# Mamba recurrence of a four-layer network: chunks of 64 tokens, two side by side on the partitions, in place of chunks of 128

## What is computed

```python
dt = softplus(dt + dt_bias)
a  = exp(dt * -exp(A_log))                      # one decay per token and head
db = dt[..., None, None] * x[..., None] * Bh[:, :, :, None, :]
states = associative_scan(a2*s1 + s2, (a, db))  # along the tokens
y = einsum('blhps,blhs->blhp', states, Ch) + D_param * x
y = y * silu(z); y = group-normed over 256 features; out = y @ W_out + b_out
```

## Time and profile before

| | |
|---|---|
| median of 3 runs | 2790.08 us (2783.35 to 2790.38) |
| the profiled execution: own time, span | 2787.64 us, 2785.9 us |
| PE busy | 2633.5 us (95% of the span), 13426 matmul records |
| DVE (VectorE) busy | 1671.9 us (60%) |
| ACT (ScalarE), POOL (GpSimd) busy | 1069.7 us (38%), 944.4 us (34%) |
| mean granted TensorE clock | 0.973 of full speed |

### The profile page before, as it was taken

The page is one execution under the profiler, slowest core; times in us unless marked ns, Lnnn a source line. Parts: engine busy times, 40 slices in busy tenths (PEclk is TensorE's granted clock), DMA queues, the critical chain, the costliest instruction groups (busy, mean ns, idle before and its releaser), DMA issues.

```text
span 2785.9 us, 35158 instructions
## 1 busy us (share of the span) xinstructions
PE 2633.5 (95%) x13426; PEld 1670.9 (60%) x13426; DVE 1671.9 (60%) x3408; ACT 1069.7 (38%) x1954; POOL 944.4 (34%) x921
## 2 busy tenths in 40 slices
PE   7988988999999999999999998889999999979996
PEld 4445544664656556566566565646666666756896
DVE  6676672227575664755763324678888988844323
ACT  2534552114444443544444112433444444332221
POOL 3221210003232231322321003426767767754222
PEclk8999999999999999999999999979999999989998
DMA  6222211017000000000000200000000000035123
GB/s 189 62 61 64 60 46 61 0 46 105 1 1 1 1 1 1 1 1 1 0 16 1 105 0 31 1 16 12 16 16 12 16 13 16 13 125 191 58 73 135
DMA packets 57112, 109.11 MB, mean 39 GB/s; under 512 B 13792, under 2 KB 32480, under 8 KB 55792
## 3 DMA queue, kind: packets, MB, share of 16 engines
q1 hardware_dynamic: 53152, 96.47, 12.4%
q0 software_dynamic: 3792, 10.39, 1.0%
HBM read 71.16 MB, written 27.08 MB: 35 GB/s over the span
## 4 chain that ended last, share of the span: by engine, by line
PE 87%; DVE 7%; ACT 2%; issue 1%; DMA 1%; POOL 1%; SPq 1%; POOLq 0%; DVEq 0%; ACTq 0%
PE ps L1256 9%; PE ps L1238 8%; PE ps L1771 5%; PE ps L1247 5%; PE ps L1228 5%; PE ps L1812 4%; PE ps L378 4%; PE ps L1265 4%; PE ps L360 4%; PE ps L365 4%; PE ps L1874 4%; PE ps L2889 3%; PE ps L2913 3%; PE ps L697 2%; PE ps L721 2%; PE ps L1840 2%
## 5 line engine op out<-in xcount | busy, mean ns | idle before, releaser
L1256 PE MATMUL ps<-back 128*128 128x512 f32 x576 | 292.0, 596 | 0.3 <-ACT back L1299 0.3
L1299 ACT ACTIVATE back<-ps 128x512 f32<-128x512 f32 x288 | 170.1, 597 | 266.2 <-PE ps L1247 264.5
L1294 ACT ACTIVATE back<-ps,front 128x128 f32<-128x128 f32 (+7 forms) x256 | 189.1, 739 | 71.7 <-DVE front L1345 70.0
L1388 POOL TENSOR_TENSOR back<-back 128x512 f32<-128x512 f32 x72 | 91.4, 1270 | 362.0 <-DVE back L1333 361.9
L1247 PEld LDWEIGHTS ps<-front,back 128*128 128x128 f32 x1152 | 140.8, 141 | 118.4 <-issue 95.0
L1398 POOL TENSOR_SCALAR back<-back,front 128x128 f32<-128x128 f32 (+5 forms) x192 | 142.5, 746 | 191.3 <-DVE front L1364 188.5
L809 ACT ACTIVATE back<-ps 128x1024 f32<-128x1024 f32 (+1 forms) x192 | 150.8, 811 | 128.2 <-PE ps L721 127.7
L1345 DVE TENSOR_REDUCE front<-ps 128x1 f32<-128x128 f32 (+7 forms) x256 | 194.0, 758 | 8.8
L1974 DVE TENSOR_TENSOR_SCAN back<-ps,back 128x512 f32<-128x512 f32 x128 | 155.9, 1218 | 50.4 <-PE ps L1784 50.1
L1338 DVE TENSOR_TENSOR ps<-ps,front 128x128 f32<-128x128 f32 x256 | 76.1, 297 | 165.8 <-PE ps L1238 165.8
L1247 PE MATMUL ps<-front,back 128*128 128x128 f32 x1152 | 170.5, 273 | 3.4 <-DVE back L1370 3.4
(11 more groups left out here) (319 smaller groups left out, 5694.1 us busy)
## 6 DMA issues: line engine op xcount, KB each, us to landing
whole<-l_w SPq DMA_DIRECT2D x32, 512.0 KB, 5.2
front<-back SPq DMA_DIRECT2D x128, 64.0 KB, 2.0
rounded<-qh SPq DMA_DIRECT2D x28, 256.0 KB
rounded<-kh SPq DMA_DIRECT2D x56, 128.0 KB
front<-xg SPq DMA_DIRECT2D x47, 129.0 KB
xg<-front SPq DMA_DIRECT2D x2, 3008.0 KB, 35.8
front<-l_win SPq DMA_DIRECT2D x1, 4640.0 KB, 17.7
front<-l_wgu SPq DMA_DIRECT2D x2, 2048.0 KB, 13.5
```

What stands on the lines that cost most here:

```text
L1256: e.matmul(PS[:, 7, :], self.V[:, j, G % 4 * 128:G % 4 * 128 + 128], self.turned(("turn", n, j)), start=(j == 0), stop=(j == qt)).then_inc ...
L1294: e.activation(self.P[n % 2][:, h, :nk], s[:, :nk], ACT.Exp, bias=st[:, 0, h:h + 1], scale=1.0, accum_out=st[:, 1, h:h + 1]).then_inc(A.se ...
L1299: e.activation(self.turned(step), self.bank(step), ACT.Copy).then_inc(A.sem, 1)
```

## The change

The chunks get 64 tokens. Two chunks of 64 (s = 0, 1) that were one chunk of 128 lie on partitions 0 to 63 and 64 to 127 of LT, XD, Bd and CB, so each table of decays is 64 x 64 and LT, CB and the scan's width are halved. There are 8 states per n instead of 4, kept in 8 buffers.

- scan: two steps per n instead of four, each two matmuls of 256 columns (one per head) into one bank and one scan of 128 x 512. New weights `selA` pick a chunk's half for each half of the partitions; GpSimd builds them together with `selP` (for cp), 768 columns per two n instead of 128, at an earlier place.
- cb: 8 matmuls with 64 columns of weights and 64 moving instead of 4 of 128 x 128. The copy and the products with LT have half the width.
- st: 8 chunks, weights 64 x 32, in two steps: s = 0 at place 0.05, s = 1 at 0.2, with a gate and an out step between them. h waits for the second.
- within: two steps of 16 matmuls (weights 64 x 64, 64 columns moving), at 0.25 and 0.35, with xd, cb and a gate step between them.
- across: 8 chunks of 64 columns. h: 8 instructions instead of 4, the same size each.
- cp: two matmuls of 256 columns instead of one of 512.
- `MambaSteps`: eight copies of 32 x 256 and sixteen scans of 64 x 64. The identity is built with one instruction instead of four.

```diff
         "pe": {"raw": (-2.5, -2),
-             "scan": (-1.1, -1, -0.8, -0.6), "st": (0.05,), "within": (0.25,), "across": (0.6,),
+             "scan": (-1.1, -0.8), "st": (0.05, 0.2), "within": (0.25, 0.35), "across": (0.6,),
...
         "dve":
-             "scan": (-1, -0.8, -0.65, -0.5), "h": (0.2, 0.3, 0.3, 0.5),
+             "scan": (-1, -0.65), "h": (0.2, 0.2, 0.3, 0.3, 0.3, 0.3, 0.5, 0.5),
...
             elif kind == "scan":
-                e.matmul(p, m.pair[:, hh:hh + 1].broadcast_to([128, 128]), m.R[:, tok], start=True,
-                         stop=True).then_inc(P.sem, 1)
+                for j in range(2):
+                    t = e.matmul(p[:, 256 * j:256 * j + 256], m.selA[g % 2][:, 2 * step[2] + j, :], m.Ra[:, cols],
+                                 start=True, stop=True)
...
             elif kind == "cb":
-                    t = e.matmul(p[:, i * 128:i * 128 + 128], m.BC[q, g // 4, o], m.BC[q, 2 + g // 4, o], start=True,
+                    for s in range(2):
+                        t = e.matmul(p[64 * s:64 * s + 64, i * 64:i * 64 + 64], m.BC[q, g // 4, o],
+                                     m.BC[q, 2 + g // 4, o], start=True, stop=True)
...
             elif kind == "st":
+                q = slice(64 * s, 64 * s + 64)
                     for h in range(4):
-                        t = e.matmul(S[32 * h:32 * h + 32, i, :], m.Bd[:, i, h, :],
+                        t = e.matmul(S[32 * h:32 * h + 32, 2 * i + s, :], m.Bd[q, i, h, :],
...
             elif kind == "within":
                     for h in range(4):
+                        s = h // 2 if step[2] == 0 else 1 - h // 2
+                        q = slice(64 * s, 64 * s + 64)
-                        t = e.matmul(net.PS[r, self.Y[h // 2], v], m.XD[:, c, h * 64:h * 64 + 64], m.LT[:, h, c, :],
+                        t = e.matmul(net.PS[r, self.Y[h // 2], v], m.XD[q, c, h * 64:h * 64 + 64],
+                                     m.LT[q, c4, h, i, :], ...)
...
             elif kind == "across":
-                for i in range(4):
+                for i in range(8):
...
             elif kind == "h":
-                w.wait_ge(self.products, self.pn["st", n])
+                w.wait_ge(self.products, self.pn["st", n, 1])
```

More of the change, by code:

```diff
@@ L1439, in __init__ @@
         self.Crep = sb(WA0 + 15936, 1024)
-        self.sel = [net.sbr(R0 + 128 * i, 128) for i in range(2)]
-        self.ident4 = sb(EX0, 512)
+        self.ident8 = sb(EX0, 512)
         self.dt = sb(EX0 + 512, 16, 32)
@@ L1496, in __init__ @@
         self.wide = net.sb(WA0 + 13376 + 512 * 5, 512)
-        self.rows = net.sb(WA0 + 16448, 2048)
+        self.rows = net.sb(WA0 + 16448, 1024)
     def pe_begin(self, e, w):
@@ L1630 @@
     AT = {
-        "pe": {"raw": (-2.5, -2), "scan": (-1.1, -1, -0.8, -0.6), "xd": (-0.75, -0.6), "cp": (-0.2,),
-             "cb": (-0.74,), "st": (0.05,), "within": (0.25,), "across": (0.6,), "gate": (0.15, 0.3), "var": (1.45,),
+        "pe": {"raw": (-2.5, -2), "scan": (-1.1, -0.8), "xd": (-0.75, -0.6), "cp": (-0.2,),
+             "cb": (-0.74,), "st": (0.05, 0.2), "within": (0.25, 0.35), "across": (0.6,), "gate": (0.15, 0.3), "var": (1.45,),
              "out": (1.85, 2.2)},
@@ L1781, in pe @@
             elif kind == "scan":
-                hh = 4 * g + step[2]
                 p = self.take(w, step, self.B)
-                e.matmul(p, m.pair[:, hh:hh + 1].broadcast_to([128, 128]), m.R[:, tok], start=True,
-                         stop=True).then_inc(P.sem, 1)
+                w.wait_ge(self.pooled, self.gn["sel", n // 2 * 2])
+                for j in range(2):
+                    t = e.matmul(p[:, 256 * j:256 * j + 256], m.selA[g % 2][:, 2 * step[2] + j, :], m.Ra[:, cols],
+                                 start=True, stop=True)
+                t.then_inc(P.sem, 1)
             elif kind == "xd":
@@ L1795, in pe @@
                 p = self.take(w, step, self.B)
-                w.wait_ge(self.pooled, self.gn["sel", n // 2 * 2])
-                e.matmul(p, m.sel[g % 2], m.R[:, tok], start=True, stop=True).then_inc(P.sem, 1)
+                for s in range(2):
+                    t = e.matmul(p.rearrange("p (i s t) -> p s i t", i=4, s=2)[:, s], m.selP[g % 2][:, s, :],
+                                 m.Rp[:, cols], start=True, stop=True)
+                t.then_inc(P.sem, 1)
             elif kind == "cb":
@@ L1831, in pe @@
                 w.wait_ge(self.results, self.dn["xd", n, 1])
+                if step[2]:
+                    w.wait_ge(P, self.pn["within", n, 0])
                 if n > 0:
@@ L1972, in dve @@
                 if n > 1:
-                    w.wait_ge(self.products, self.pn["within", n - 2])
-                e.tensor_tensor_scan(m.LT[:, h, four, :].rearrange("p a b -> p (a b)"), self.bank(step, self.B),
-                                     m.ident4, 0.0, ALU.mult, ALU.add).then_inc(D.sem, 1)
+                    w.wait_ge(self.products, self.pn["within", n - 2, 1])
+                e.tensor_tensor_scan(m.LT[:, c4, 2 * h:2 * h + 2].rearrange("p h a b -> p (h a b)"), self.bank(step, self.B),
+                                     m.ident8, 0.0, ALU.mult, ALU.add).then_inc(D.sem, 1)
             elif kind == "xd":
@@ L1989, in dve @@
                     w.wait_ge(self.products, self.pn["across", n - 2])
-                    for i in range(4):
+                    for i in range(8):
                         if not self.last_chunk(n - 2, i):
                             w.wait_ge(D, self.dn["h", n - 2, i])
-                e.tensor_copy(m.ach[:, four], p[:, 127:512:128])
+                e.tensor_copy(m.ach[:, 8 * c4:8 * c4 + 8], p[:, 63:512:64])
                 w.wait_ge(self.crep[c4], 64 * (n // 2 + 1))
@@ L1996, in dve @@
             elif kind == "bd":
-                for h in range(4):
+                for h in range(2):
                     w.wait_ge(D, self.dn["scan", n, h])
@@ L2012, in dve @@
                 st = self.state(n, i)
-                w.wait_ge(self.products, self.pn["st", n])
-                if st > 3:
-                    w.wait_ge(self.products, self.pn["across", self.reader(st - 4)])
-                new, old = m.H[st % 4], m.H[(st - 1) % 4]
+                w.wait_ge(self.products, self.pn["st", n, 1])
+                if st > 7:
+                    w.wait_ge(self.products, self.pn["across", self.reader(st - 8)])
+                new, old = m.H[st % 8], m.H[(st - 1) % 8]
                 if c4 + i == 0:
@@ L2068, in pool @@
                     w.wait_ge(self.products, self.pn["cp", n - 3])
-                e.tensor_copy(m.sel[g % 2].rearrange("p (a b) -> p a b", a=4),
-                              m.pair[:, 32 + 4 * g:36 + 4 * g].unsqueeze(2).broadcast_to(
-                                  [128, 4, 32])).then_inc(G.sem, 1)
+                both = m.pair.rearrange("p (s h) -> p s h", s=2)[:, :, 4 * g:4 * g + 4]
+                e.tensor_copy(m.selA[g % 2].rearrange("p h (s t) -> p h s t", s=2),
+                              both.rearrange("p s h -> p h s").unsqueeze(3).broadcast_to([128, 4, 2, 64]))
+                e.tensor_copy(m.selP[g % 2].rearrange("p s (h d) -> p s h d", h=4),
+                              both.unsqueeze(3).broadcast_to([128, 2, 4, 32])).then_inc(G.sem, 1)
             elif kind == "cb":
```

108 lines of the change are left out of this document (60 added, 48 removed), and 4 rows, old and new, of the table AT.

## The result

The changed kernel takes 2756.52 us (median of 4 runs, 2753.76 to 2761.73). The kernel before, in the same comparison, takes 2788.6 us (2783.35 to 2790.38). The ratio is 0.989, with a 95% interval of 0.9869 to 0.9911. So the change makes the kernel some 30 us faster. The profiled execution after took 2753.76 us, 33.9 us less than that of before.

What follows compares the result with a forecast made beforehand. The prediction took PE, busy for 95% of the span, as the bound. −19 (PE) + 6.5 (stalls) − 2 (first two n) − 1.5 (stage before) = −16 us gave 2774 us for the median, range 2761 to 2799.

Steps and rivals of the forecast that it cites:

- PE's terms in the steady part: PE's blocks scan, cb, within, st, across and cp: sum −0.59 us per n, −19 us over 32 n.
- The open price: Time per 64-column record in 64 × 64 tiles, shown by no row: bounds 14 and 27 ns, 14 taken.
- The rival of tiles that don't run four abreast: within and across cost 27 ns a record: 2819 us, or 2844 with st too; chance 0.10 for both.
- the stall: PE waits 0.35 us before its second xd for DVE's scan, in 16 + 3 n: +6.5 us.
- The rival in which DVE holds the even n: Late second st delays h and bd: 2789 us with one more slow tap, 2803 with two; chance 0.22 for 2782 to 2800.
- its walk: DVE and PE followed through an even n: second st at 4.23, DVE idle 1.9 us, bd done at 14.5.
- Its rival without a stall: DVE's taps fall beside less GpSimd work, PE gets its full 19 us, the start 4: 2764 us; chance 0.10.
- The first two n ... −2 us (0 to −5): Start of the stage, not PE-bound: fewer scans and half of cb, against one stall for the second st: −2 us.
- The stage before ... −1.5 us: `MambaSteps` pieces, half copies and half-length scans: −0.5 us for each of three of four pieces, −1.5 us (0 to −4).

Runs made afterwards that it cites:

- after_pad: The changed kernel with one more VectorE instruction (a sum over 1024 columns) in each even n, ahead of a scan: 2811.56 us, ratio 0.9996 to the kernel before.
- before_cb64: The kernel before with only cb's matmuls as in the change, 8 of 64 x 64 per n: 2797.97 us against 2813.61, ratio 0.9951.
- before_short_products: The kernel before with the sixteen running-product scans of the stage before over 64 columns instead of 128: 2778.0 us, ratio 0.9978.
- before_warm_n1: The kernel before with 7 extra matmuls, results never read, in PE's 3.5 us pause at n = 1: 2783.96 us, ratio 0.9994.
- before_pad: The kernel before with one more VectorE instruction at the place of its third scan in each even n: 2815.17 us, ratio 1.0008.

## Why the forecast was right and wrong

**Right: PE's terms in the steady part.** In an n without a stall PE takes 0.58 us less (18.35 to 17.77), where the sum said 0.59. Its parts can be read in the rows above: cb 0.61 to 0.62 (0.60), within 2 × 0.62 (1.35 with both entries), st 0.58 and 0.59, across 1.09 and 0.98 (1.0 for 60 records). The open price, 64 × 64 tiles as two row halves by two column halves, fits 14 ns, the lower of the two bounds: within's blocks of 32 records take 0.62 us, less the fixed 0.15 that is 15 ns each. across takes 0.11 us for its 8 extra records. The rival of tiles that don't run four abreast is out. The Trainium skill's page "TensorE: Matmul & The Clock Gate" (section "Wait — 56ns, not 53.3ns?") gives some 25 ns as the least from start to start; for tiles side by side the trace doesn't agree, with 14 ns in runs of 64 records.

**Right in kind, less in size: the stall.** DVE stands still for 2.14 us before the first h, as walked through. The stall of PE before the second xd is 0.36 us in two n of each group with a B and C convolution, as priced, but about 0.08 in the common even n (0.70 instead of 0.62 until xd). It was put at 0.35 everywhere. In all that is 6 × 0.36 + some 13 × 0.08, or 3 us, not 6.5. The rival in which DVE holds the even n was near: `after_pad` shows no room at all. In its walk the prediction has out at 1.73 us by the earlier trace rows, where the rows have 1.54 to the scan behind it; the place of the second st came out all the same, 4.22 us after the first (4.23). Its rival without a stall is given as 2764 us, and its own terms (−19 − 4 − 1.5, from 2790.1) make 2765.6.

**The step that failed: "The first two n ... −2 us (0 to −5)", which has no term for the clock.** The prediction read the granted clock of 0.79 in these 40 us and used it only to say that they are different. It asked for the clock only between 1900 and 2400 us, where it is 1.00 before and after, so the sum has the clock at nothing, without a reason. Between the last up block and the second across the clock was worth 8.5 us to the kernel before, and the changed kernel gets 6 to 8 of them (10.2 between the two profiles of the table). This is shown as to place, and by single traces as to size, by filling the pauses. Why the clock comes back earlier after a pause of the same 3.33 us stays open: `before_cb64`, which does the same work up to there as the kernel before, has the 48 matmuls in 10.21 us, and `before_short_products` has them in 12.66. No run here shows how its size could have been told beforehand, so that it fell on the side of the gain is luck.

**Smaller misses: the start at equal clock and `MambaSteps`.** At equal clock the start measures −4.5, where the forecast has −3.2 with these two n's share of the −19. It was read off no chain: the four small waits and the cb blocks of this stretch were never walked through as the even n was. "The stage before ... −1.5 us" measures −2.7. Its price was mis-sized: four scans of half length take 0.83 us, not 1.7.

Put together, from the windows: −12.9 in the middle, −2.7 for `MambaSteps`, −4.5 for the start at equal clock, and 6 to 8 for the clock, −26 to −28 us. The ratio says −30.7 with an interval of 24.8 to 36.5. The 3.0 us of the table behind the across of n = 31 have no cause shown: there two profiles of the kernel before differ by 4 us among themselves (306.2 and 302.3).

## What to carry to other kernels

Do one part of a change alone in thought before costing all of it: here the halved cb, a few lines, is worth the whole steady gain, and the second st blocks and the stall eat what the rest brings. Where a profile shows a stretch in which PE waits and the granted clock is below 1.00, put a term for the clock into the sum, priced by the same block at both levels in the rows; fill the pause once to learn what is at stake, and compare stretches as well as whole runs, since what lies behind can hide a few us. A wait that joins two separated blocks (h for the second st) is paid wherever the engine behind it has no slack, so put the blocks side by side first.

## What the runs showed of the hardware

- Small matmuls run four abreast at 14 ns a record with 64 columns moving: tiles of 64 × 32 (st, 0.58 us for 32 records, 0.47 for 24) and of 32 × 64 (across, 1.09 for 64, 0.98 for 56). Those of 64 × 64 in two row halves by two column halves (within, 0.62 for 32) fit the same price.
- After a pause of 3.33 us, the same 48 matmuls took 7.29 us with the pause filled, and 8.75, 10.21, 11.42, 11.58 and 12.66 us with it unfilled, in kernels that differ elsewhere. A kernel repeats its own value closely, on both chips: 11.42 and 11.58 in the two profiles of before, 11.51 and 11.48 in `before_warm_n1` and `before_pad`, 8.75 and 8.73 in the two of the changed kernel.
- A running product over 64 partitions and 64 columns takes 0.21 us; one over 32 partitions and 128 columns took 0.60.
